# A four-layer graph network on one core: layer 1's forward neighbour sums taken from gathered source rows instead of from dense weight matrices

## The reference

```python
def _weighted_mean_agg(ft, w, src, dst, n_nodes):
    m = ft[src] * w[:, None]
    msum = segment_sum(m, dst, n_nodes)
    wsum = segment_sum(w, dst, n_nodes)
    safe = where(wsum > 0, wsum, 1.0)
    return where((wsum > 0)[:, None], msum / safe[:, None], 0.0)

neigh1 = _weighted_mean_agg(feat, w, src, dst, n)   # forward: sums at the edge's destination
neigh2 = _weighted_mean_agg(feat, w, dst, src, n)   # backward: sums at the edge's source
hn = concat([neigh1 @ W1.T, neigh2 @ W2.T])
# then a gated unit: r, z = sigmoid(...), candidate = tanh(...), out = cand + z * (feat - cand)
```

## Time and profile before

| what | value |
|---|---|
| median of 3 runs | 10153.24 us (10148.71 to 10154.86) |
| the profiled execution | 10154.51 us, of which the span is 10152.8 us |
| PE / PEld busy | 90% / 73% of the span |
| DVE / ACT / POOL busy | 57% / 46% / 32% |
| stage of the lists | span start to about 112 us |
| stage of the sums (74 batches) | about 112.85 to 3447 us |
| stage of the gated unit | 3448 to about 3670 us |

### The profile page before, as it was taken

One profiled execution on the slowest core, in us unless ns is written; L12 is line 12 of the kernel. 1 busy time (PEld: TensorE's weight loads), 2 busy tenths in 40 slices (PEclk: granted clock), 3 DMA queues, 4 the chain that ended last, 5 costly groups with the idle time before them and its releaser, 6 DMA issues. The chain is left out here.

```text
span 10152.8 us, 237386 instructions
## 1 busy us (share of the span) xinstructions
PE 9102.2 (90%) x62443; PEld 7436.0 (73%) x62444; DVE 5836.0 (57%) x12039; ACT 4659.0 (46%) x11625; POOL 3272.2 (32%) x3463
## 2 busy tenths in 40 slices
PE   6999999999999869999897788888887599999998
PEld 5999999999999747777565566666665476666666
DVE  7666666666666457776212455555554455555555
ACT  3333333333333244444101476776775455555555
POOL 2000000000000000000000477777774377777775
PEclk7999999999999889999898899999999799999999
DMA  2000000000000002222453444444442122222222
GB/s 78 3 3 3 3 3 3 3 3 3 3 3 3 11 37 110 114 114 101 167 193 118 142 118 118 118 118 118 118 118 89 50 73 73 73 73 72 72 73 69
DMA packets 372611, 702.00 MB, mean 69 GB/s; under 512 B 102415, under 2 KB 268371, under 8 KB 352468
## 3 DMA queue, kind: packets, MB, share of 16 engines
q0 software_dynamic: 136128, 335.76, 11.8%
q1 hardware_dynamic: 236052, 359.58, 10.1%
HBM read 546.68 MB, written 148.25 MB: 68 GB/s over the span
## 5 line engine op out<-in xcount | busy, mean ns | idle before, releaser
L1603 POOL DMA_INDIRECT x<-table,p_gidx x1632 | 1542.3, 945 | 2458.7 <-ACT p_gidx L1640 1990.6
L2104 POOL DMA_INDIRECT c_G<-table,c_gidx x1632 | 1555.7, 953 | 505.4 <-issue 493.1
L687 PE MATMUL g_ps_cell<-g_kw,g_loh 128*128 128x98 f32 x9472 | 1240.6, 275 | 93.0 <-DVE g_kw L617 47.3
L662 ACT COPY g_AT<-g_ps_turn 128x384 f32<-128x384 f32 (+1 forms) x1258 | 578.8, 466 | 1580.5 <-PE g_ps_turn L717 1580.5
L687 PEld LDWEIGHTS g_ps_cell<-g_kw,g_loh 128*128 128x128 f32 x9472 | 1168.0, 194 | 102.1 <-issue 71.9
L697 PE MATMUL g_ps_slot<-h,g_A 128*128 128x129 f32 x7252 | 1056.8, 282 | 56.2 <-issue 56.2
L579 POOL DMA_INDIRECT g_hrow<-table,dst_tab x74 | 69.8, 943 | 3192.4 <-PE g_ps_rev L708 3191.9
L1694 PE MATMUL p_ps_sum<-x 128*96 128x256 f32 x3264 | 893.0, 397 | 177.1 <-DVE hid L1629 164.7
L602 DVE TENSOR_TENSOR x<-x,g_ps_rev 128x387 f32<-128x387 f32 (+1 forms) x1258 | 670.8, 538 | 649.0 <-PE g_ps_rev L708 649.0
L708 PE MATMUL g_ps_rev<-g_hrow,g_AT 128*128 128x129 f32 x7252 | 1032.7, 281 | 0.5 <-ACT g_AT L662 0.5
L697 PEld LDWEIGHTS g_ps_slot<-h,g_A 128*128 128x128 f32 x7252 | 923.1, 194 | 59.0 <-issue 59.0
(11 more groups left out here) (343 smaller groups left out, 15544.7 us busy)
## 6 DMA issues: line engine op xcount, KB each, us to landing
adj_save<-a_A SPq DMA_DIRECT2D x74, 1568.0 KB, 5.1
a_A<-adj_save SPq DMA_DIRECT2D x74, 1568.0 KB, 6.6
c_ed<-in_edge_dram SPq DMA_DIRECT2D x1632, 25.0 KB
x<-table,p_gidx POOLq DMA_INDIRECT x1632
p_lhs<-in_edge_dram SPq DMA_DIRECT2D x1632, 16.0 KB
c_G<-table,c_gidx POOLq DMA_INDIRECT x1632
table<-m_rows SPq DMA_DIRECT2D x17, 384.0 KB, 2.5
x<-in_x_dram SPq DMA_DIRECT2D x1, 3328.0 KB, 11.0
```

The lines of the kernel that those rows point to most:

```text
L662: s.copy(AT[:, b, 0:w], ps_turn[b][:, 0:w]).then_inc(at_ready, 1)
L687: last = pe.matmul(ps_cell[q % 2][:, r * KEYS:(r + 1) * KEYS], loh[:, b, cell, :], kw[:, b, cell, :], start=True, stop=True)
L1603: g.indirect_dma_start(G[:, H * b + q, :], None, table2, bass.IndirectOffsetOnAxis(ap=gidx[:, b, q:q + 1], axis=0)).then_inc(gathered[b], 16)
L2104: g.indirect_dma_start(G[:, H * b + q, :], None, table, bass.IndirectOffsetOnAxis(ap=gidx[:, b, q:q + 1], axis=0)).then_inc(gathered[b], 16)
```

## The change

1. The forward sums no longer use `A` or `h`. Edges are regrouped into "runs" of RQ = 4 tiles; RPB = 6 runs belong to a batch, 444 in all. For each tile of a run, GpSimd gathers the 128 source rows of `table` (one indirect DMA). ACT multiplies them by the edge weights and makes a one-hot of the destinations; PE adds up one-hot times rows over the 4 tiles in PSUM; DVE adds the result to one bucket of `fwd`.
2. `forward`, its placing matmuls, `place_hot`, the copies into `sums` and the counts go. `A` serves the backward sums only.
3. `stage_lists` also makes the list of runs (`run_tab`, saved to DRAM and read back per batch) and no longer counts edges.
4. `h` is not kept in SBUF; `stage_gru_nodes` reads it back from `table` by chunk (`hin`). The means are made two chunks ahead instead of one.

```diff
+RQ = 4
+RT = -(-ET // RQ)
+RPB = -(-(RT + BUCKETS - 1) // NBATCH)
+GR = 3
+OH_AT = {0: 0, 2: 1, 5: 2, 8: 3, 10: 4, 13: 5}
+SCALE_AT = {1: 0, 4: 1, 6: 2, 9: 3, 12: 4, 14: 5}
+RUN_AT = {2: 0, 5: 1, 7: 2, 10: 3, 13: 4, 15: 5}
+ADD_AT = {3: (0, 0), 6: (0, 1), 8: (0, 2), 11: (0, 3), 14: (0, 4), 0: (-1, 5)}
...
 # stage_lists: vector, scalar
-                            for j in range(GRP):
-                                last = v.tensor_reduce(cnt_c[:, j, g0:g0 + m], here[:, j, 0:m, :], AX_X, ALU.add)
-                            then(last)
+                            if which == 2:
+                                v.tensor_copy(key_g, e[:, :, 0, :])
+                                v.tensor_scalar(low_g, e[:, :, 1, :], start[:, 2 * LG + g0:2 * LG + g0 + 1], None, ALU.subtract).then_inc(keys_made, 1)
+                                continue
...
 # stage_gru_sums: sync
+                        def load(i, bb):
+                            n = 2 * i + bb
+                            if not (isinstance(n, int) and n < 2):
+                                sp.wait_ge(weighted, RPB * (n - 1))
+                            sp.dma_start(runs[:, bb, :, :], run_save[:, :, bass.ds(n * RD, RD)]).then_inc(runs_in[bb], 16)
...
 # gpsimd
+                        for n in range(NBATCH):
+                            if n >= 2:
+                                g.wait_ge(rev_made, TGS * (n - 1))
+                            g.indirect_dma_start(hrow[:, n % 2, 0:D], None, table,
+                                                 bass.IndirectOffsetOnAxis(ap=dst_tab[:, n % 2, n // 2:n // 2 + 1], axis=0)).then_inc(gathered[n % 2], 16)
+                            g.wait_ge(runs_in[n % 2], 16 * (n // 2 + 1))
+                            for e in range(RPB):
+                                m = RPB * n + e
+                                if m >= GR:
+                                    g.wait_ge(weighted, m - GR + 1)
+                                for q in range(RQ):
+                                    g.indirect_dma_start(G[:, e % GR, q, 0:D], None, table,
+                                                         bass.IndirectOffsetOnAxis(ap=runs[:, n % 2, 0, RQ * e + q:RQ * e + q + 1], axis=0)
+                                                         ).then_inc(rows_in[e % GR], 16)
...
 # vector
+                        def add_run(n, s):
+                            if s not in ADD_AT:
+                                return
+                            back, e = ADD_AT[s]
+                            ...
+                            m = RPB * (n + back) + e
+                            at = bass.ds(run_bucket(v, n + back, e), 1)
+                            v.wait_ge(run_made, m + 1)
+                            v.wait_ge(added, m + 1)
+                            v.tensor_tensor(fwd[:, at, :], fwd[:, at, :], ps_run[e % 2][:, 0:D + 2].rearrange("p (o d) -> p o d", o=1),
+                                            ALU.add).then_inc(added, 1)
...
 # scalar; in step q, after the copies of A and AT: make_run_oh if q in OH_AT, weigh_run if q in SCALE_AT
+                        def make_run_oh(i, n, bb, e):
+                            m = RPB * n + e
+                            if e == 0:
+                                s.wait_ge(runs_in[bb], 16 * (i + 1))
+                            if not (isinstance(m, int) and m < 2):
+                                s.wait_ge(run_made, m - 1)
+                            for q in range(RQ):
+                                last = s.activation(roh[:, e % 2, q, :], iota, ACT.Abs, bias=runs[:, bb, 1, RQ * e + q:RQ * e + q + 1].bitcast(F32), scale=-1.0)
+                            last.then_inc(away, 1)
+                            s.wait_ge(away, m + 1)
+                            s.activation(roh[:, e % 2, :, :], roh[:, e % 2, :, :], ACT.Relu, bias=1.0, scale=-1.0)
+                        def weigh_run(n, bb, e):
+                            s.wait_ge(rows_in[e % GR], 16 * RQ * (RPB // GR * n + e // GR + 1))
+                            for q in range(RQ):
+                                last = s.activation(Gw[:, e % 2, q, 0:D + 1], G[:, e % GR, q, :], ACT.Identity,
+                                                    scale=runs[:, bb, 2, RQ * e + q:RQ * e + q + 1].bitcast(F32))
+                            last.then_inc(weighted, 1)
...
 # tensor
-                                if known(n - 1):
-                                    forward(n - 1, 1 - bb, q)
...
-                                if q == 6 and known(m):
-                                    pe.wait_ge(summed, m + 1)
-                                    pe.wait_ge(poh_ready, m + 1)
-                                    for k in range(GRP):
-                                        last = pe.matmul(ps_slot[bb][:, k * (D + 2):(k + 1) * (D + 2)], poh[:, bb, k * P:(k + 1) * P], sums[:, bb, :],
-                                                         start=True, stop=True)
-                                    last.then_inc(placed, 1)
+                        def sum_run(n, e):
+                            m = RPB * n + e
+                            pe.wait_ge(weighted, m + 1)
+                            if not (isinstance(m, int) and m < 2):
+                                pe.wait_ge(added, m)
+                            for q in range(RQ):
+                                last = pe.matmul(ps_run[e % 2][:, 0:D + 2], roh[:, e % 2, q, :], Gw[:, e % 2, q, :], start=q == 0, stop=q == RQ - 1)
+                            last.then_inc(run_made, 1)
+                                if known(n) and q in RUN_AT:
+                                    sum_run(n, RUN_AT[q])
...
 # stage_gru_nodes: sync, tensor, vector
                         for c in range(NCH):
                             if c >= 2:
+                                sp.wait_ge(turned, c - 1)
+                            sp.dma_start(hin[:, c % 2, 0:count(c), :], tiles(table)[:, tiles_in(c), :]).then_inc(h_in[c % 2], 16)
+                            if c >= 2:
                                 sp.wait_ge(added, c - 1)
                             sp.dma_start(xin[:, c % 2, 0:count(c), :], a["x"][:, tiles_in(c), :]).then_inc(x_in[c % 2], 16)
...
                             pe.wait_ge(means_ready, 2 * c + 2)
+                            pe.wait_ge(h_in[c % 2], 16 * (c // 2 + 1))
...
                         means(0)
+                        means(1)
                         for c in range(NCH + 2):
-                            if c + 1 < NCH:
-                                means(c + 1)
+                            if c + 2 < NCH:
+                                means(c + 2)
```

More of the change, by code:

```diff
@@ L234, in stage_lists @@
                 groups = [(0, g0, min(LP, LG - g0)) for g0 in range(0, LG, LP)] + [(1, g0, min(LP, PG - g0)) for g0 in range(0, PG, LP)]
+                groups += [(2, g0, RQ) for g0 in range(RG)]
                 before = [sum(m for _, _, m in groups[:k]) for k in range(len(groups) + 1)]
                 def ends_seen(k):
-                    return ends_in[k % RING], 16 * sum(groups[j][2] for j in range(k % RING, k + 1, RING))
+                    return ends_in[k % RING], 16 * sum(1 if groups[j][0] == 2 else groups[j][2] for j in range(k % RING, k + 1, RING))
                 with nc.Block() as block:
@@ new lines, in _ @@
+                        then(v.tensor_scalar(whole[:, TK:2 * TK], whole[:, TK:2 * TK], 683.0, None, ALU.mult))
+                        then(v.tensor_scalar(whole[:, TK:2 * TK], whole[:, TK:2 * TK], 11, None, ALU.arith_shift_right))
+                        then(v.tensor_copy(first[:, :], whole[:, :]))
+                        v.wait_ge(consts, 10)
+                        then(v.tensor_tensor(first[:, :], first[:, :], tno[:, :], ALU.add))
+                        for at in columns:
+                            last = v.memset(first[0:1, at.start:at.start + 1], 0.0)
@@ L332, in _ @@
                         then(last)
-                        for k in range(2):
+                        for k in range(3):
                             last = v.tensor_tensor(base[:, k, :], number[:, :], tix[:, k, :], ALU.subtract)
@@ L449, in _ @@
                         for t in range(NT):
[L450 removed]
+                            s.activation(h[:, t, :], x[:, t, :], ACT.Relu, bias=nmr[:, t:t + 1], scale=rstd[:, t:t + 1]).then_inc(normed, 1)
                         for k, (which, g0, m) in enumerate(groups):
@@ L461, in _ @@
                                 s.copy(w_tab[:, cols], pt[at % 4][:, 2 * P:3 * P]).then_inc(taken, 1)
-                            if which == 0 and g0 + m == LG:
-                                s.wait_ge(cnts_turned, 1)
-                                for j in range(GRP):
-                                    last = s.copy(cnts[:, :, j, :], ps_cnts[0:LG, j * P:(j + 1) * P].rearrange("g (h c) -> g h c", h=2))
-                                last.then_inc(cnts_made, 1)
-                        s.wait_ge(small_turned, 2)
```

(18 more changed lines are left out.)

231 lines of the change are left out of this document (123 added, 108 removed).

## The result

The changed kernel takes 10283.26 us (median of 4 runs, 10273.58 to 10298.32) against 10154.05 (4 runs, 10148.71 to 10178.76) for the kernel before: ratio 1.0124, 95% interval 1.0103 to 1.0145. It is slower, as forecast, by 1.2%; 10320 had been predicted. The profiled execution took 10286.65 us (span 10284.9), 132.1 more than the profiled one of before. By stage: lists +12.0 (112.85 to 124.84), sums +104.1 (3335.1 to 3439.2), gated unit +16.6 (217.6 to 234.2). The sums start with the first GpSimd instruction of their block, the gated unit and the layer behind it with SP's first load. Layers 2 to 4 take the same time, within 0.6 us.

What follows compares the result with a forecast made beforehand. PE was taken to bound the sums at 0.111 us per instruction. 10154.5 + 146 (sums) + 0 (first and last batches) + 2 (lists) + 17 (gated unit) = 10320 us, slower; range 10130 to 10480.

Steps and rivals of the forecast that it cites:

- The new wait: Sums: run 0's gathers queue behind GpSimd's wait for hrow; PE may start at T0 + 9.6, pausing 5.6 us every batch.
- T0: Sums: end of the last backward group in step 0 of a batch, which ends GpSimd's wait before gathering hrow.
- The clock: Sums: half clock expected behind each 5.6 us pause, losing 1.7 to 3.1 us per batch, 2.4 taken.
- Rival A: Sums: the pause is there but the clock stays up; pair 89.6, total 10148 us, no change; chance 8%.
- PE's saving: Sums: 323 PE instructions per batch instead of 377, 36.0 us, 6.0 less; loop jump still costing 5.2 a pair.
- ACT: Sums: ACT has 31.7 us per batch against PE's 36.0; its bursts pause PE 0.6 us per batch (0 to 1.2).
- rival C: Sums: ACT becomes the bound, small activations at L450's price; pair 98.7, total 10475 us; chance 13%.
- The pair: Sums: two batches take 94.4 us against 90.3, +4.1 for 36 pairs, +146 us (+13 to +313).
- The first and last batches: Sums' ends: first two batches gain runs but lose forward, last body loses forward; together 0 (-8 to +6) us.
- The lists: Lists stage: edge counts go, 11.5 us; 16 more tiles and a longer save come; +2 us (-6.5 to +8.5).
- The gated unit: Gated unit: early means leave PE's path, but turn waits for hin behind xin: 3.5 us, +17 in all (+3 to +28).
- Rival B: Sums: run 0's rows are there in time and PE's saving arrives; pair 79.6, total 9785 us; chance 5%.

Runs made afterwards that it cites:

- e4: Changed kernel without run sums (no row gathers, one-hots, weighing, run matmuls, adds); forward sums uncomputed: 11485 us on chip A (before: 12395), pair 63.10.
- e12: e1 with rows gathered for the first three runs only and reused, all other run work kept: 9739 us on chip D, 0.9588 of before, pair 77.04.
- e11: e4 with 16 row gathers per batch put back, read by nobody: 9208 us on chip D, 0.9065 of before, pair 63.10.
- e3: e1 with PE's loop alone holding four batches a pass instead of two: 12805 us on chip A, 1.0329 of before (e1: 12784).
- e10: The kernel with both edits, with run gathers between the two kinds of tile gathers in the lists: 12706 us on chip C, 1.0243 of before.
- e8: The kernel with both edits, run on chip C: 12670 us, 1.0204 of before, pair 99.0.
- e9: e8 with the gated unit's means one chunk ahead again: 12768 us on chip C, 1.0301 of before.
- the kernel with both edits: e1 plus hin of chunk c+1 issued ahead of xin of chunk c: 1.0227 of before on chip A, 1.0106 on B, 1.0204 on C.
- e1: Changed kernel with GpSimd's wait for backward sums and hrow gather moved behind the gathers of runs 0 to 2: 12784 us on chip A, 1.0320 of before.
- run 2: Not an experiment: a batch's third edge run, counted from 0; hrow gathered behind it is e1's order, 12784 us on chip A, 1.0320 of before.

## Why the prediction was right, step by step

The stage of the sums, per pair (means of 34; the single pairs lie between 89.0 and 90.9 before, 63.0 and 63.1 in e4, 76.9 and 77.3 in e12, 91.9 and 93.4 in the changed kernel): 89.80 before; forward and its work removed 26.70 (to 63.10, e4 and e11); run sums' work 13.94 more (to 77.04, e12); gathers in the changed order 15.16 more (to 92.20). The last step holds both the gathers and their order; on a chip like that of the result the order alone was not run.

* **The new wait, right.** T0 to the first run matmul is 10.26 us in the mean of 72 batches (forecast 9.6), the pause 5.4 (5.6). From the start of run 0's last gather to ACT it is 2.6 (2.8). The two first run gathers took 1.28 and 1.72 us instead of 0.94, which I had not counted, and PE itself reached the wait at T0 + 4.8 instead of 4.0. These two misses cancel in the pause.
* **The clock, right in kind, too dear.** Half speed behind every pause. Against e12, the eight run instructions lose 0.94 us and the eight of the cells 0.62 (1.65 against 1.03): about 1.6 where 2.4 was taken, below even my low end of 1.7. The stretch at half clock was about as long as that of rows 7 (6.8 us against 6.3), but I charged half of all of it: at the jump the clock fell 0.9 us ahead of the pause's end, here 3.6 us, so only 3.2 us at half clock are left for PE's work. And the 4 us of idle time that I read in rows 6 are two pauses with 1.1 us of work between them. Pause and clock together: 2 x (5.4 + 1.6) = 14.0 of the 15.16 a pair, where 16.0 was forecast; the other 1.2 are not settled. Rival A is out; it would have needed a clock of 1.0.
* **PE's saving, right, but the jump was the step that failed.** The step read "The jump costs 6.35 less what of its slow stretch lies behind T0 ...: 5.2"; I took it for a cost of the jump, and e3 shows that it is one of the body's length. Nothing of it was left. In numbers: 102 instructions a batch at 0.1114 are 22.7 us a pair, but 26.7 went. Before, the jump cost 89.80 - 84.0 = 5.8 a pair in the mean: the waits of PE from 1016 to 3048 us, in 22.6 passes, make 3.5 of it (the two rows below and 11.6 us for DVE); the half clock behind them is taken to be the rest. Without it 2 x 275 x 0.1114 = 61.3 would be left. 63.10 is measured; 1.2 of the 1.8 between them is a wait for DVE's adds that the sum had at nothing. The rows are of the kernel before, then of e11 from 500 to 1500 us, 15.8 pairs:

```profile
PE g_ps_slot L697 <- issue: 36.7, 22, 1.9
PE g_ps_cell L687 <- issue: 30.3, 15, 2.3
```

```profile
PE g_ps_rev L786 <- DVE x L663: 19.7, 32, 0.7
```

* **ACT, right.** PE waits 0.8 us a batch for its copies (0.6 forecast), and rival C is out: four weighings took 1.28 us (1.3 forecast, 1.64 by the rival). The two sums for ACT in the prediction come to 11.6 and 7.8 us and not 11.3 and 7.5, which changes nothing. The runs' work in all cost 13.9 a pair where 10.7 + 1.2 were forecast; what the other 2.0 are is not settled.
* **The pair, in part luck.** Without pause and clock it was forecast at 72.0 + 5.2 + 1.2 = 78.4, and e12 has 77.04. The jump's 5.2 never came; 1.8 and 2.0 us that the sum did not have, and 0.4 more for ACT, stood in for most of it.
* **The first and last batches, wrong.** 0 (-8 to +6) was forecast. From the start of the stage to the third `hrow` it is 7.2 us more, and from `hrow` of batch 72 to the end 7.4: both ends now hold runs (the 35 pairs between them make up the other 89.5), and the tail's chain of turn, copy and backward, 1.83 us a step, gains hardly anything from forward's removal. The stage came out nearer to its forecast by this: 36 pairs of 2.4 more are 86 us, not 146.
* **The lists, wrong: +12.0, forecast +2 (high end +8.5).** The runs' part was sized right: the last save goes out 14.6 us behind the save of the edge lists (100.39), where 13.5 were forecast; in them DVE waited 1.6, 1.7 and 5.2 us for the last three gathers. What failed is the step "The edge counts go ... 11.5 us of DVE's path". Three of the nine groups stood ahead of a wait that DVE has in both kernels; it grew from 3.8 to 7.9 us, and from its end to the save of the edge lists only 7.5 us went (48.93 to 41.45). Two terms had been put at nothing: all up to that wait is 3.5 us later, for a reason that is open, and the last save takes 1.4 us longer to let the stage end (9.9 against 8.5). 3.5 - 7.5 + 14.6 + 1.4 = 12.0. e10 shows that moving the gathers is no cure.
* **The gated unit, right: +16.6, forecast +17**, by the mechanism named: in the middle chunks the turn follows 3.5 to 4.1 us behind the add's end, where it was 2.03 (forecast 3.5). The early means were "hidden behind a load", as the prediction says, and e8 and e9 show what they are worth without it: 81 us.

So +104.1 + 12.0 + 16.6 against +146 + 2 + 17. Rival B, rows in time, was not what this kernel does; e12, with 77.04 against the rival's 79.6, shows what the stage would take if the rows cost nothing. On a chip like D, e12 and e11 together (pair 77.04, gathers free of charge beside PE) and the gated unit's 99 us less point to about 9640 us for the kernel with both edits, 5% below before. That is an estimate, 9739 - 99, and not shown. It leaves little room: at the changed kernel's mean of 1.16 us a run gather and 0.30 between two, 24 of them and `hrow` take GpSimd 36.3 of the 38.5 us of such a batch, while e11 had 16, unread. The kernel with both edits only came to chips A, B and C, where it is the best changed one, and still 1.1 to 2.3% slower than before.

## What to carry to other kernels

In an in-order list, look at what stands behind a new or old wait: one gather that nobody needed for a whole batch held 24, the first four of which were needed at once, and the same pattern (a load queued behind another load's wait) turned a good prefetch into a loss. Cost a removal in instructions and in code length: a loop body that becomes short enough is no longer fetched in each pass, and its fetch pauses go as well. And time a kernel that leans on GpSimd gathers on more than one chip.

## What the runs showed of the hardware that was not expected

**Chips differ where rows are gathered.** The code behind the gated unit is the same in e4 and e11; it takes 8742 us on chip A (span 11483.3, last add at 2741.7) and 6472 on D (9206.0, 2734.3). e4's sums, with one gather a batch, take the same 63.10 there. With run gathers, ACT on chip A passes waits late. In e1, PE's backward and turn had ended at 2015.48 and 2015.80 and ACT's copy before at 2015.98; the copy that needs no more than these starts at 2018.72, beside GpSimd's gathers ("remote" is an event without a recorded source):

```profile
2014.62 0.86 PE L783 MATMUL g_ps_rev<-g_hrow,g_AT 128*128 128x129 f32 x6
...
2015.31 0.49 PE L794 MATMUL g_ps_turn<-ident,g_A 128*128 128x128 f32 x3
...
2015.51 0.47 ACT L739 COPY g_A<-g_ps_cell 128x392 f32<-128x392 f32 x1
...
2016.70 1.71 POOL L635 DMA_INDIRECT g_G<-table,g_runs  x1 [0.30 <-issue]
...
2018.72 0.48 ACT L749 COPY g_AT<-g_ps_turn 128x384 f32<-128x384 f32 x1 [2.74 <-remote]
```

From 1016 to 3048 us PE waited 214 to 316 us for such copies on A, B and C, in the kernels with `hrow` behind run 2, against 34.5 in the changed kernel on the chip of the result. That gathers cause it is argued from their lying side by side, and not shown: e11, which could have told, ran on chip D.

**A gather's issue is longer beside one DVE instruction.** In the changed kernel, from 500 to 3400 us, the 378 run gathers that lie beside L687 (`kw`, a float32 by a bfloat16 operand, 0.97 us) take 1.66 us in the mean. The 344 beside L681 and L684 but not L687 take 1.10, the other 788 take 0.95. A gather that starts 0.07 us into L687 ends 0.82 us behind its end, as if it had waited for it. The Trainium skill, "SBUF — State Buffer", "SBUF: two separate sides", tells of a port pair of DVE and GpSimd that a DVE instruction with two SBUF inputs locks for its whole length, against a GpSimd instruction that reads SBUF. The trace agrees for L687. L684, 1.22 us long, also has two SBUF inputs and costs a gather 0.15 us, and L681 alone costs nothing (34 gathers, 0.95), so by these rows the lock does not hold for every such instruction. No run took L687 away, so the cause stays argued.
